# Integer weights for a quarter of eight blocks of a dequantized expert on one Trainium2 core

## The reference, cut to what matters

```
x = x + _layernorm(_L0_attn_ref(_layernorm(x), ...))   # a state-space scan
x = x + _layernorm(_L0_ffn_ref(_layernorm(x), ...))    # the expert
x = x + _layernorm(_L1_attn_ref(_layernorm(x), ...))   # attention over 16 dimensions of one token
x = x + _layernorm(_L1_ffn_ref(_layernorm(x), ...))    # a mixture layer
...
w[k,n] = q[k,n]*s[g,n] - (z[g,n]+1)*s[g,n],  g = k // groupsize     # groupsize 128
gate = x2 @ Wg ; up = x2 @ Wu                                       # 512 -> 1376
inter = gate * jax.nn.sigmoid(gate) * up
out = (inter @ Wd).astype(jnp.float16)
```

## Time and profile before

| | us |
|---|---|
| median of 3 runs (802.38 to 802.8) | 802.54 |
| the profiled execution, its own time | 807.23 |
| its span on the core | 805.3 |
| PE, DVE, ACT, POOL busy | 683.3, 684.8, 470.1, 481.6 |
| mean granted TensorE clock | 0.916 of full |
| batch 0's expert on PE | about 486 to 576 |
| batch 1's expert on PE | 576 to 670.7 |
| mixture layer and its tail | 670.7 to 805 |

### The profile page before, as it was taken

One profiled execution on the slowest core, in us unless ns is written; L12 is line 12 of the kernel. 1 busy time (PEld: TensorE's weight loads), 2 busy tenths in 40 slices (PEclk: granted clock), 3 DMA queues, 4 the chain that ended last, 5 costly groups with the idle time before them and its releaser, 6 DMA issues. The chain is left out here.

```text
span 805.3 us, 8451 instructions
## 1 busy us (share of the span) xinstructions
PE 683.3 (85%) x2794; PEld 323.7 (40%) x2794; DVE 684.8 (85%) x697; ACT 470.1 (58%) x805; POOL 481.6 (60%) x252
## 2 busy tenths in 40 slices
PE   7979889987776888555546879999999999999995
PEld 6623333322121332111111324444445456887885
DVE  6869999999999999999999998998274565585778
ACT  5468787895755675867664547757325347323333
POOL 2419999999999999999999970220002014341130
PEclk9989989999878999558857999999999999999998
DMA  8434133334502715630334309962040030000011
GB/s 261 94 92 151 43 115 104 131 130 141 206 24 87 244 60 170 229 131 27 104 131 160 121 1 284 265 190 64 0 157 1 1 105 0 1 1 1 0 53 52
DMA packets 42358, 83.19 MB, mean 103 GB/s; under 512 B 6825, under 2 KB 10340, under 8 KB 42060
## 3 DMA queue, kind: packets, MB, share of 16 engines
q1 hardware_dynamic: 42316, 82.67, 32.1%
HBM read 71.44 MB, written 11.21 MB: 103 GB/s over the span
## 5 line engine op out<-in xcount | busy, mean ns | idle before, releaser
L2403 POOL TENSOR_TENSOR dbu<-rep_du,bc 128x1024 f32<-128x1024 f32 x127 | 296.8, 2365 | 2.2 <-DMA bc<-bc_scratch 1.0
L1895 ACT ACTIVATE psum<-rep_dt,aneg 128x512 f32<-128x512 f32 x256 | 166.1, 682 | 116.9 <-DVE hc L1245 94.3
L1234 DVE TENSOR_TENSOR_SCAN psum<-psum,dbu 128x1024 f32<-128x1024 f32 x89 | 203.3, 2285 | 3.4 <-POOL dbu L2403 1.6
L985 PE MATMUL psum<-hc,stk 128*32 128x512 f32 x512 | 83.4, 728 | 60.5 <-POOL hc L2412 41.6
L1245 DVE TENSOR_TENSOR hc<-psum,bc 128x1024 f32<-128x1024 f32 x89 | 108.9, 1224 | 3.1
L2412 POOL TENSOR_TENSOR hc<-hc,bc 128x1024 f32<-128x1024 f32 x39 | 92.1, 2362 | 6.1 <-DVE hc L1234 6.0
L1234 DVE TENSOR_TENSOR_SCAN hc<-psum,dbu 128x1024 f32<-128x1024 f32 x39 | 88.9, 2280 | 1.6 <-ACT psum L1895 0.9
L719 PE MATMUL psum<-xf_hi,gu_lo 128*128 128x512 f16 x176 | 67.5, 383 | 0.0
L719 PE MATMUL psum<-xf_hi,gu_hi 128*128 128x512 f16 x176 | 67.4, 383 | 0.1
L719 PE MATMUL psum<-xf_lo,gu_hi 128*128 128x512 f16 x176 | 67.3, 383 | 0.0
L719 PE MATMUL psum<-xT,w_g 128*128 128x512 f32 x120 | 59.7, 647 | 2.6 <-ACT rep_du L2040 2.6
(11 more groups left out here) (301 smaller groups left out, 1444.3 us busy)
## 6 DMA issues: line engine op xcount, KB each, us to landing
rep_dt<-rep_scratch SPq DMA_DIRECT2D x60, 256.0 KB, 3.4
rep_du<-rep_scratch SPq DMA_DIRECT2D x60, 256.0 KB, 4.3
cw<-c_scratch SPq DMA_DIRECT2D x11, 768.0 KB, 8.2
qw<-qgu_in SPq DMA_DIRECT2D x11, 512.0 KB, 6.4
bc<-bc_scratch SPq DMA_DIRECT2D x16, 256.0 KB, 4.6
rep_scratch<-du_t SPq DMA_DIRECT2D x14, 256.0 KB, 2.0
rep_scratch<-dt_t SPq DMA_DIRECT2D x14, 256.0 KB, 2.3
qw<-qd_in SPq DMA_DIRECT2D x11, 256.0 KB, 6.8
```

The source lines that it names most:

```text
L985: last = pe.matmul(y_rows(k), stk[:], hc[:, (i + k // 2) % HCS, k % 2, :], start=False, stop=(s == GN - 1))
L1234: dve.tensor_tensor_scan(h, a, dbu[:, i % DBS].rearrange("p e t -> p (e t)"), 0.0, ALU.mult, ALU.add)\
L1895: last = act.activation(psum[:, 2 * (i % 2) + e, :], rep_dt[:, cc % 2, k, :], ACT.Exp, scale=aneg[:, k, c, n:n + 1])
L2403: pool.tensor_tensor(dbu[:, i % DBS], rep_du[:, cc % 2, k:k + 2, :], bc[:, n, :].unsqueeze(1).broadcast_to([P, 2, L]), ALU.mult).then_inc( ...
```

## The change

In blocks 1, 2, 3, 4, 6, 7, 8 and 9 of batch 1's expert (`GROUPED`), the last quarter of the input is multiplied by the whole numbers q - zero, which a 16-bit float holds exactly, so two matmuls do in place of three. They go to bank 4, and the scale is applied afterwards, for each output row: ACT scales the bank into `sg` (gate) or `it` (up), and DVE adds the other three quarters' product. The whole numbers are copied by SP from the staging slot before it is loaded again, and the scales are loaded as a column for each block.

```diff

+GROUPED = (1, 2, 3, 4, 6, 7, 8, 9)
...
+            def keep_ints(i):
+
+                if i not in GROUPED:
+                    return
+                sp_.wait_ge(q16_used, i + 1)
+                sp_.dma_start(ints[i][:], cw[i % SLOTS][:, 0, 2 * (KH - 1) * P:2 * KH * P]).then_inc(ints_kept, 16)
...
+                if i > SLOTS:
+                    sp_.wait_ge(ints_kept, 16 * kept_up_to(i - SLOTS))
...
             stage(3)
+            keep_ints(1)
...
+                def group_part(i, j):
+
+                    n = 2 * GROUPED.index(i) + j
+                    if n:
+                        pe.wait_ge(group_done, n)
+                    else:
+                        pe.wait_ge(ints_kept, 16 * len(GROUPED))
+                    w = ints[i][:, j * P:(j + 1) * P]
+                    pe.matmul(psum[:, Y_BANK, :], w, xf_hi[1][:, KH - 1, :], start=True, stop=False)
+                    pe.matmul(psum[:, Y_BANK, :], w, xf_lo[1][:, KH - 1, :], start=False, stop=True)\
+                        .then_inc(group_ready, 1)
...
-                        for kk in range(KH):
+                        for kk in range(KH - 1 if grouped else KH):
...
+                        if grouped and j == 0:
+                            group_part(i, 0)
                         product(item, parts).then_inc(work_ready, 1)
+                        if grouped and j == 1:
+                            group_part(i, 1)
...
+            def norm_last(layer, t):
+
+                if layer == "moe":
+                    wait_work(dve, ("tr", "att", 1, t))
+                dve.tensor_scalar(xnd[:, t, :], x[:, NT + t, :], mean_of((layer, 1), t), rstd_of((layer, 1), t),
+                                  ALU.subtract, ALU.mult).then_inc(xn_ready, 1)
...
+            def gate_sum(i):
+                k = IC + i
+                item = ("g", 1, i)
+                wait_work(dve, item)
+                dve.wait_ge(group_done, 2 * GROUPED.index(i) + 1)
+                dve.tensor_tensor(sg[:, k % 2, :], bank(item), sg[:, k % 2, :], ALU.add).then_inc(taken_sem(item), 1)
+
+            def up_sum(i):
+                k = IC + i
+                item = ("u", 1, i)
+                wait_work(dve, item)
+                dve.wait_ge(group_done, 2 * GROUPED.index(i) + 2)
+                dve.tensor_tensor(it[:, k % 2, :], bank(item), it[:, k % 2, :], ALU.add).then_inc(taken_sem(item), 1)
+
+            def times_sum(i):
+                k = IC + i
+                dve.wait_ge(silu_done, GROUPED.index(i) + 1)
+                wait_taken(dve, ("u", 1, i))
+                dve.tensor_tensor(it[:, k % 2, :], sg[:, k % 2, :], it[:, k % 2, :], ALU.mult).then_inc(it_done, 1)
...
                 link(dve.tensor_reduce(smax[:], sc[:], AX.X, ALU.max))
+                if b == 0:
+                    gate_sum(6)
...
                 dve.tensor_reduce(num[:], sc[:], AX.X, ALU.add)
+                if b == 0:
+                    gate_sum(7)
...
+            dve.wait_ge(ld_att, 16 * 7)
+            dve.tensor_reduce(wqkv[:, :, 0:DH], wqraw[:], AX.X, ALU.add).then_inc(wq_done, 1)
+            dve.tensor_reduce(bqkv[:, 0:DH], bqraw[:], AX.X, ALU.add).then_inc(wq_done, 1)
+            dve.wait_ge(ld_group, 32)
+            dve.tensor_copy(group32[:], group16[:]).then_inc(group_set, 1)
             for i in range(IC):
+                if i in GROUPED and i not in (6, 7, 8):
+                    gate_sum(i)
                 if i == IC - 1:
                     low_moe(0, [2, 3])
-                ffn_times(1, i)
+                if i in GROUPED:
+                    up_sum(i)
+                    if i == 1:
+                        ffn_inv16(0)
+                        ffn_add16(0, 0)
+                    times_sum(i)
+                else:
+                    ffn_times(1, i)
                 if i == 9:
                     norm_tile("moe", 0, 2, xnc)
                     norm_tile("moe", 0, 3, xnc)
+                if i in (0, 1, 3, 4):
+                    between(0, i)
                 ffn_low(1, i)
-                if i == 0:
-                    dve.wait_ge(ld_att, 16 * 7)
-                    dve.tensor_reduce(wqkv[:, :, 0:DH], wqraw[:], AX.X, ALU.add).then_inc(wq_done, 1)
-                    dve.tensor_reduce(bqkv[:, 0:DH], bqraw[:], AX.X, ALU.add).then_inc(wq_done, 1)
-                if i < 8:
+                if i in (2, 5, 6, 7):
                     between(0, i)
                 if i == 7:
+                    gate_sum(8)
                     between(0, 8)
                 if i == 8:
                     inv_std(("moe", 0), NT)
@@ -1638,14 +1759,6 @@
                 last.then_inc(taken_sem(item), 1)
...
+            def group_scaled(i, j):
+
+                k = IC + i
+                if i == 1:
+                    act.wait_ge(group_set, 1)
+                act.wait_ge(group_ready, 2 * GROUPED.index(i) + j + 1)
+                if j:
+                    act.wait_ge(itlo_done, k - 1)
+                act.activation((it if j else sg)[:, k % 2, :], psum[:, Y_BANK, :], ACT.Identity,
+                               scale=group32[:, j, i:i + 1]).then_inc(group_done, 1)
+
+            def ffn_silu_sum(i):
+
+                k = IC + i
+                wait_taken(act, ("g", 1, i))
+                act.activation(sg[:, k % 2, :], sg[:, k % 2, :], ACT.Silu).then_inc(silu_done, 1)
...
-                ffn_silu(k)
+                if b == 1 and i in GROUPED:
+                    if i - 1 not in (0, 2, 5, 6, 8):
+                        group_scaled(i, 1)
+                    ffn_silu_sum(i)
+                else:
+                    ffn_silu(k)
...
+                if b == 1 and i + 1 in GROUPED and i != 5:
+                    group_scaled(i + 1, 0)
                 ffn_high(k)
...
+                    if i in (2, 5, 6, 8):
+                        act.preload_act_table_set(LOG_EXP)
+                    if i == 8:
+                        root(("moe", 0), NT)
+                    if i == 5:
+                        group_scaled(i + 1, 0)
+                    if i in (0, 2, 5, 6, 8):
+                        group_scaled(i + 1, 1)
                     if i == 0:
                         root16(0)
-                    if i in (2, 5, 6, 8):
-                        act.preload_act_table_set(LOG_EXP)
                     if i == 2:
                         root(("att", 0), NT)
                     if i == 5:
                         att_exp(0)
                     if i == 6:
                         root(("atto", 0), NT)
```

More of the change, by code:

```diff
@@ L680, in _ @@
             load(bet[:], beta_in.broadcast_to([P, H]), ld_att)
+            keep_ints(IC - 2)
+            for j in range(2):
+                sp_.dma_start(group16[:, j, :], sgu_in[2 * (KH - 1) + j:2 * KH - 1 + j, :]
+                              .rearrange("r (i n) -> n (r i)", n=P),
+                              allow_slow_non_contiguous=True).then_inc(ld_group, 16)
             sp_.wait_ge(wq_done, 2)
@@ L710, in turn @@
                 pe.wait_ge(xn_ready, XN[item[1:]] + 1)
-                n = t if (layer, b) == ("ffn", 1) else XN[item[1:]] % 2
+                n = t if b and layer != "ssm" else XN[item[1:]] % 2
                 for k in range(KH):
@@ L1528, in att_add, with h2_low @@
                 link(last)
+            def h2_low(b, i):
+                k = b * MI + i
+                dve.wait_ge(h2hi_done, k + 1)
+                if b == 1 and i == MI // 2:
+                    wait_work(dve, ("routed", b, NT - 1))
+                dve.tensor_tensor(h2_low_of(b, i), h2[:, k % 2, :], h2_high_of(b, i).bitcast(F32),
+                                  ALU.subtract).then_inc(h2lo_done, 1)
             def between(b, i):
@@ L1544, in between @@
                     inv_std(("att", b), NT)
-                    norm_tile("att", b, 0, xnc)
-                    norm_tile("att", b, 1, xnc)
-                if i == 4:
+                    if b:
+                        for t in range(NT):
+                            norm_last("att", t)
+                    else:
+                        norm_tile("att", b, 0, xnc)
+                        norm_tile("att", b, 1, xnc)
+                if i == 4 and b == 0:
                     norm_tile("att", b, 2, xnc)
@@ L1685, in _ @@
             for i in range(MI):
-                h2_low(0, i)
+                if i:
+                    h2_low(0, i)
                 if i == 0:
                     between(1, 3)
-                    between(1, 4)
                 if i in (2, 3, 4, 5):
@@ L1693, in _ @@
                     inv_std(("moe", 1), NT)
-                    norm_tile("moe", 1, 0, xnc)
-                    norm_tile("moe", 1, 1, xnc)
-                if i == 7:
-                    norm_tile("moe", 1, 2, xnc)
-                    norm_tile("moe", 1, 3, xnc)
+                    for t in range(NT):
+                        norm_last("moe", t)
             low_moe(1)
```

73 lines of the change are left out of this document (50 added, 23 removed).

## The result

| | before | after |
|---|---|---|
| median of 10 runs (lowest to highest), us | 804.53 (802.38 to 807.81) | 807.89 (805.8 to 809.8) |
| the profiled execution, its own time and span, us | 807.23, 805.3 | 807.92, 806.0 |
| PE, DVE, ACT busy, us | 683.3, 684.8, 470.1 | 676.3, 694.7, 480.3 |

What follows compares the result with a forecast made beforehand. PE was taken as the bound, with no waits in batch 1's expert. Savings of 5.4 us against new stalls of 5.6 gave +0.2, rounded to +0.3 on 802.54: 802.8 us, range 800.0 to 805.2.

Steps and rivals of the forecast that it cites:

- Sum of what goes: PE time removed: matmuls 3.46, first tile's early norm 0.4, block 2's SiLU 0.2, `h_lo` 0.6, four buffers 0.7; 5.4 us.
- With `h2_low(0, 0)` ahead of a statistics group the 0.6 goes: Mixture layer: moving the first tile's subtraction ahead of statistics removes PE's 0.6 us wait for `h_lo`.
- the early tile: The first tile's early norm removes PE's 0.4 us wait for the first tile of a norm.
- place one: Block 1 of batch 1's expert: `it_lo` ends at E + 13.3, E being block 0's issue end; stall 1.2 us.
- place two: Down(7): block 6's scaling delays the exponential and block 7's gate sum adds 0.6; stall 1.6 us, partly perhaps at block 8.
- place three: Down(8): block 8's gate sum adds 0.6, its up sum and linked product 0.65; stall 2.3 us.
- place four: Transpositions behind block 9: two more DVE operations ahead of the tiles and `xm_lo`; stall taken as 0.5 us.
- rival (a): The clock falls behind the new stalls: 1.7 us each, 804.5 us for one and 806.2 for two; chance 0.15.
- Rival (b): Copies of whole numbers hold up staging loads: at a cost of 2 to 3 us, 805 us; chance 0.08.
- Rival (c): Chains are shorter than counted and half the stalls are absent: 2.8 us less, 800.0 us; chance 0.15.
- Rival (d): The clock's fall behind the attention product goes away: 801.1 us; chance 0.08.
- cushion of 2.5 us: Batch 1's expert before the change: block 8's `it_lo` ends 2.5 us before PE asks for it at down(8).

Runs made afterwards that it cites:

- small_edits: The changed kernel without whole numbers (no copies, scale loads, scalings or sums), keeping only the other edits: 0.9994 of the time before.
- four_h2_back: Whole numbers in blocks 2, 3, 4 and 9 only, with the mixture layer's early subtraction put back behind the statistics: 0.9963 of the time before.
- four_blocks: The changed kernel with whole numbers in blocks 2, 3, 4 and 9 only: 0.998 of the time before.
- after_again: The changed kernel run and profiled a second time, nothing changed: 808.65 us.
- after_third: The changed kernel run and profiled a third time, nothing changed: 806.76 us.
- copies_by_gpsimd: The changed kernel with the eight copies of whole numbers issued from GpSimd's queue in place of SyncE's: 1.0032 of the time before.
- adds_behind: The changed kernel with the reciprocal and three additions of batch 0's tiles moved behind block 1's `it_lo`: 1.0045 of the time before.
- before_again: The kernel before run and profiled once more, nothing changed: 804.39 us.
- copies_only: The kernel before plus only the eight copies, two small scale loads and the staging loads' waits on the copies, results unread: 1.001 of the time before.
- without_six: The changed kernel with block 6 in full products again, the other seven blocks keeping whole numbers: 1.0053 of the time before.
- block_eight_too: Whole numbers in blocks 2, 3, 4, 8 and 9, with the early subtraction put back: 0.9976 of the time before.

## Why the prediction was wrong

The forecast was 0.3 us more, and 3.5 were measured. Three terms make up the 3.2 between them, to within what the runs can tell: 1.6 in the mixture layer, 0.9 in the waits of batch 1's expert, and 0.9 for the clock on the mean.

*Sum of what goes, 5.4 us: some 1.6 too much.* The matmuls (3.46) are right, and the SiLU's 0.2 is a little small (0.38 in small_edits, since a second gap of 0.13 goes too). The step that failed is "With `h2_low(0, 0)` ahead of a statistics group the 0.6 goes". The wait did go. But the working never asked what the statistics do: behind them stand the square root, the norm and the turned tiles, and PE was already waiting for those. In the trace above the subtraction holds them back by 1.6 us: 0.21 in which DVE waits for its input, and the 1.49 of the subtraction, which takes 0.69 where GpSimd is idle. 0.6 gained and 1.6 lost make the 0.96 of four_h2_back against four_blocks. The other 0.4, the early tile, goes as well (0.41 before, no wait for `obuf` after), but batch 0's expert varies by more than that.

*Places one to four: the right waits, 6.5 us in place of 5.6.* Measured from start to start: place one 1.4 (predicted 1.2), place two 0.52 + 1.14 (1.6), place three 2.8 (2.3), place four about 0.6 (0.5). The chain was right in its moments too: with Q at 624.59 block 7's `it_lo` ends at 645.62 = Q + 21.0, which is Q + 22.7 less the 1.7 of the fall that did not come. Place three was mis-sized by a link: 0.04 was taken from `ffn_add16`, 0.46 stood there. Of the rest 0.2 is in place one, where `it_lo` ends at E + 13.5 in place of E + 13.3.

*The clock, rival (a), given 0.15.* It has come true behind down(8) in four of the five profiles with all eight blocks: after_again, after_third, copies_by_gpsimd and adds_behind, but not the first of after. It falls in none of the others, with waits of 2.30 or 1.32 or none. The argument against it, "around the waits of 2.1 and 1.4 us at the scan's end the granted clock stays 1.00", rested on one execution: in all thirteen other profiles the clock does fall around there (0.83 to 0.91 in 470 to 490). The stretch in before, then in before_again, the clock again behind the five busy times:

```profile
470.00:490.00 20.00, 15.60 (x62) 5.33 (x61) 19.32 (x22) 10.18 (x17) 8.06 (x4) 1.00 0.36 97
470.00:490.00 20.00, 16.29 (x58) 6.09 (x58) 17.64 (x22) 9.76 (x16) 5.26 (x3) 0.83 0.41 110
```

The Trainium skill, TensorE: Matmul & The Clock Gate, in its section on a second failure mode, tells of a kernel that cycles through PSUM banks, idles briefly between its groups and is throttled again and again. These runs agree as far as they go: PE waits 1.25, 0.35, 0.98 and 2.64 us (in adds_behind 0.25, 1.06, 0.37, 0.98 and 2.29), and then the granted clock is 0.50, which is 1.2 GHz, in four profiles of five. Which of the waits matters, and how long it must be, no run here tells: the falls were counted, not caused.

*Rival (b), given 0.08.* Waits for staged loads are there in some profiles, without the copies too. The price is not settled: +0.8 with an interval of -0.5 to +2.0 us in copies_only.

*Rival (c)* did not come: the chains are 0.9 us longer than counted, not shorter.

*Rival (d)* took a fall in one execution for a property of the kernel. So did the cushion of 2.5 us ahead of down(8), "the number on which the change turns": in before_again, without the fall, block 8's `it_lo` ends at 652.40 and PE asks at 653.24, a cushion of 0.84. The sum of the stalls did not suffer by it, since in the changed kernel the exponential waits for PE and both sides move together.

The ledger, from before_again to the changed kernel: batch 1's expert -0.6 ahead of the attention product, +3.35 behind it, and 1.1 for the clock in four of five, 0.9; the mixture layer +0.6 and -0.3. That is 4.0, less some tenths in batch 0's expert, against 3.5 measured. What lies ahead of batch 0's expert is not in it: that expert starts at 485.78 and 485.93 in the two profiles of before and at 484.43 to 484.89 in the three of the changed kernel, but at 483.15 to 487.23 in kernels with the same scan, so that no run tells what of this the change does.

*What the profile was to show.* The waits before down(1), down(7) and down(8) and none for `h_lo`: as said. The exponential stands 5.5 us behind block 6's start, not 7, since the clock had not fallen. The mixture layer "within 1 us of the old time" holds between the first two profiles (670.94 and 670.49) by luck: before had the fall of 1.7. Batch 1's expert takes 95.4 to 96.5 us against 92.65 in before_again.

## What to carry to other kernels

Before an operation is moved forward, look at what it is moved ahead of, and follow that to its reader as well: a visible wait of 0.6 us was bought with one of 1.6. Saving matmuls in a stage with long chains on other engines pays only block by block where no chain ends: with the early subtraction in both, four blocks take 0.998 of the time before and eight 1.0044. (With it undone four take 0.9963, about 3 us less; by the stretches 1.2 of these are the whole numbers' and 1.0 the buffers' and the order's, the rest lies in batch 0's expert and in the noise.) And two profiles of a kernel tell what one cannot: which of its rows are the kernel's, and which are the clock's.

## What the runs showed of the hardware

- The same pair on DVE, block 8's up sum and the linked product behind it, stands 1.15 us from start to start in all three profiles of the changed kernel and in copies_by_gpsimd, and 0.79 in adds_behind, without_six and block_eight_too. SiLU's result was there some 2 us earlier in each. Blocks 2 and 4 of the changed kernel have 0.78 to 0.80 for their pairs. The difference is in the programs, not in the executions; its cause stays open. The Trainium skill, VectorE: DVE Perf Modes, says in its section on the drain, of eight copies with a semaphore behind each, that the semaphore costs nothing extra. Here a successor without a link starts after 0.61 us and a linked one after 0.79, 0.18 more; what the other 0.36 of the 1.15 are is not known.
- DVE's subtraction for `h_lo`, 128x512, took 0.69 us in the five of eight cases in the changed kernel in which GpSimd was idle, and 1.49 (at 688.06), 1.10 and 1.11 in the three in which a GpSimd operation was running when it started. A product of `scaled` took 2.71 at 521.78, GpSimd's addition running since 520.88, and 1.76 at 513.76, where the addition started behind it, at 514.01.
- The granted clock fell to 0.50 behind the 32 small matmuls of batch 0's attention product in two of 14 profiles (before, copies_by_gpsimd), and behind batch 1's in one of 14 (after_again): the same code, once at 1.00 and once at 0.50.
